# Attention and token-pair block on one core: jobs moved between attention tiles, and the last two tiles merged with the first token pair into one hand-ordered passage

## The reference

```
x = x + attention(layernorm(x))        # 16 heads of 32
x = x + ffn(layernorm(x))              # 512 -> 4096 -> 512, gate/up/down, 4-bit weights with scales
attention: q,k = rotate(silu(x Wq)), rotate(silu(x Wk)); v = x Wv
           per chunk of 128: o = (q k^T * D) v + (q*decay) S;  S = lam*S + (k*decay)^T v
           o = rmsnorm_per_head(o * sigmoid(x Wg1 Wg2)) * w;  out = o Wo
ffn:       (gelu(x Wg^T) * (x Wu^T)) Wd^T
```

## Time and profile before

| | us |
|---|---|
| median of 3 runs | 1325.35 (1324.91 to 1329.5) |
| profiled execution, its own time | 1327.92 |
| its span | 1325.8 |
| PE busy | 1287.1 (97%) |
| DVE busy | 945.0 (71%) |
| ACT busy, POOL busy | 475.7, 434.4 |
| mean granted clock of PE | 0.99 |

### The profile page before, as it was taken

The page is one execution under the profiler, slowest core; times in us unless marked ns, Lnnn a source line. Parts: engine busy times, 40 slices in busy tenths (PEclk is TensorE's granted clock), DMA queues, the critical chain, the costliest instruction groups (busy, mean ns, idle before and its releaser), DMA issues.

```text
span 1325.8 us, 19563 instructions
## 1 busy us (share of the span) xinstructions
PE 1287.1 (97%) x6796; PEld 1058.3 (80%) x6796; DVE 945.0 (71%) x1618; ACT 475.7 (36%) x799; POOL 434.4 (33%) x360
## 2 busy tenths in 40 slices
PE   8799999998789999999999999999999999999998
PEld 6688777886578888888888888888888888888887
DVE  7687988778666676667676676667676676767665
ACT  4333343333443323333333333333433333333331
POOL 2233554465442223232423223232413222232410
PEclk9799999998999999999999999999999999999999
DMA  9000000000010110000000010000000100100003
GB/s 318 8 1 10 12 14 1 1 2 0 1 33 16 32 32 28 27 24 24 24 32 16 32 32 24 32 24 24 24 32 16 32 31 17 38 24 24 24 9 119
DMA packets 21774, 40.17 MB, mean 30 GB/s; under 512 B 2660, under 2 KB 2916, under 8 KB 21604
## 3 DMA queue, kind: packets, MB, share of 16 engines
q1 hardware_dynamic: 21060, 39.47, 9.1%
q10 hardware_dynamic: 672, 0.13, 0.0%
HBM read 35.40 MB, written 4.19 MB: 30 GB/s over the span
## 4 chain that ended last, share of the span: by engine, by line
PE 90%; DVE 7%; issue 2%; ACT 1%; DVEq 0%; ACTq 0%
PE bank L1293 15%; PE bank L1296 15%; PE bank L1295 15%; PE bank L1151 12%; PE bank L1153 12%; PE bank L1152 12%; PE bank L1165 2%; PE bank L1241 1%; PE bank L1258 1%; DVE nt_t L597 1%; PE bank L1398 1%; DVE xol L791 1%; PE bank L1248 1%; DVE nt_t L599 1%; PE bank L1281 1%
## 5 line engine op out<-in xcount | busy, mean ns | idle before, releaser
L881 DVE TENSOR_TENSOR acc<-acc,bank 128x512 f32<-128x512 f32 x248 | 169.4, 683 | 129.2 <-PE bank L1153 129.2
L1151 PE MATMUL bank<-wdh,hh 128*128 128x512 f32 x512 | 199.3, 389 | 0.0
L1153 PE MATMUL bank<-wdh,hl 128*128 128x512 f32 x512 | 199.2, 389 | 0.0
L1152 PE MATMUL bank<-wdl,hh 128*128 128x512 f32 x512 | 199.2, 389 | 0.0
L1293 PE MATMUL bank<-xoh,wgh 128*128 128x512 f32 x448 | 175.9, 393 | 4.8 <-DVE xol L791 2.4
L1293 PE MATMUL bank<-xoh,wuh 128*128 128x512 f32 x448 | 175.1, 391 | 0.7 <-ACT cxa L494 0.7
L1296 PE MATMUL bank<-xoh,wgl 128*128 128x512 f32 x448 | 174.5, 390 | 0.0
L1296 PE MATMUL bank<-xoh,wul 128*128 128x512 f32 x448 | 174.3, 389 | 0.0
L1295 PE MATMUL bank<-xol,wuh 128*128 128x512 f32 x448 | 174.3, 389 | 0.0
L1295 PE MATMUL bank<-xol,wgh 128*128 128x512 f32 x448 | 174.3, 389 | 0.0
L897 DVE TENSOR_TENSOR hl<-hx,hh 128x512 fp32r<-128x512 f32 x128 | 114.5, 895 | 52.1 <-ACT hh L501 51.7
(11 more groups left out here) (156 smaller groups left out, 2341.5 us busy)
## 6 DMA issues: line engine op xcount, KB each, us to landing
stg<-packed_dram SPq DMA_DIRECT2D x48, 256.0 KB, 2.6
stg<-scales_dram SPq DMA_DIRECT2D x48, 256.0 KB
out_dram<-acc SPq DMA_DIRECT2D x16, 256.0 KB, 2.0
acc<-x_dram SPq DMA_DIRECT2D x3, 1024.0 KB, 14.7
w_in<-wq_dram SPq DMA_DIRECT2D x2, 512.0 KB, 5.2
w_in<-wk_dram SPq DMA_DIRECT2D x2, 512.0 KB, 6.9
w_in<-wv_dram SPq DMA_DIRECT2D x2, 512.0 KB, 8.8
w_in<-wo_dram SPq DMA_DIRECT2D x2, 512.0 KB, 11.1
```

The source lines that it names most:

```text
L881: V.tensor_tensor(row, row, BY[j % 2][:], ALU.add).then_inc(y_add, 1)
L1151: pe.matmul(dst, w_h, x_h, start=start, stop=False)
L1152: pe.matmul(dst, w_h, x_l, start=False, stop=False)
L1153: return pe.matmul(dst, w_l, x_h, start=False, stop=stop)
```

## The change

Nothing is computed differently; PE, DVE, ACT and POOL issue the same products. What is different:

1. **Jobs between tiles.** Bits, scales and parts of the three units go from tiles (4,6,8), (5,7,9), (6,8,10) to (3,6,9), (5,7,10), (6,8,11). The five bit steps stay together, ahead of `gated`. LN1 statistics: tiles 2 and 3 now ahead of the low part of x of tile 1, bn_stats of 4 to 7 in the same place before the loop, 8 to 11 aggregated in tile 4, 12 to 15 in tile 8 (before: 8 to 15 in tile 4). `norm1(2)` goes ahead of the silu of tile 1 and `wo_hi` into tile 0, behind `norm1(3)`. LN2 statistics are cut at rows 0, 8, 13, 15, 16 instead of 0, 8, 14, 16; the second part is in tile 13.
2. **Passage.** Tiles 14 and 15 and pair (0,0) are one piece of code per engine, with x1's groups spread in it. The loop of pairs starts at (0,1).
3. **x1.** The row pairs are taken in the order 2, 0, 1, 3, 4 ... 7; the first is staged in a new buffer `xst`, then `ws` and `stg` in turn, and the banks are `X1_BANKS`. Some attention results go to other banks (Wo products to bank 3, the state's product to bank 2).
4. Buffers stand in another order in memory.

```diff
-LN2_ROWS = (0, 8, 14, 16)
-UNIT_BITS, UNIT_SCALE, UNIT_PARTS = (4, 6, 8), (5, 7, 9), (6, 8, 10)
+LN2_ROWS = (0, 8, 13, 15, 16)
+X1_ORDER = (2, 0, 1, 3, 4, 5, 6, 7)
+X1_BANKS = (0, 6, 1, 0, 6, 1, 0, 6, 1, 0, 6, 1, 0, 6, 1, 0, 5, 2, 5, 2, 5, 7, 5, 7, 5, 7, 5, 7, 5, 7, 5, 6)
+UNIT_BITS, UNIT_SCALE, UNIT_PARTS = (3, 6, 9), (5, 7, 10), (6, 8, 11)
...
+            xst = sb("xst", [P, 2 * OPS * P], F32, att_w)
+        x_stage = [xst[:]] + 4 * [ws[:].rearrange("p a s m -> p (a s m)"), stg[:]]
...
@@ ACT, start @@
+            norm1(2, 2)
             silu_qk(1)
             gate_low(1)
-            norm1(2, 2)
-            wo_hi()
...
@@ DVE, start @@
+            dve.wait_ge(s_x[0], 16)
+            stats(2, 4)
+            stats_r(2, 4, 1)
             xt_lo_(1)
             gate_low(0)
...
-            dve.wait_ge(s_x[0], 16)
-            stats(2, 4)
-            stats_r(2, 4, 1)
+            dve.wait_ge(s_x[1], 16)
+            stats(4, 8)
...
@@ DVE, tile @@
-                if t == CHUNKS:
-                    stats_r(2 * CHUNKS, TILES, 3)
+                if t == 4:
+                    stats_r(8, 12, 3)
+                if t == 5:
+                    dve.wait_ge(s_x[3], 16)
+                    stats(12, 14)
+                if t == 7:
+                    stats(14, 16)
+                if t == 8:
+                    stats_r(12, 16, 4)
                 if t == 11:
                     stats2(0)
-                if t == 14:
+                if t == 13:
                     stats2(1)
...
@@ POOL, x1_sums(n), i = X1_ORDER[n] @@
+                if n >= 3:
+                    pool.wait_ge(x1t_ps, 4 * n - 4)
+                pool.wait_ge(s_r2, (1, 1, 1, 1, 2, 3, 3, 4)[i])
...
@@ DVE, new @@
+            def passage():
+                s, t = TILES - 2, TILES - 1
+                normed(s - 1)
+                decayed_q(s)
+                gate_low(t)
+                ot_lo_(s - 1)
+                rope_of(BATCH - 1, s % CHUNKS, t, t % CHUNKS)
+                masked(s)
+                x1(0, 3)
+                gated(s)
+                x1(4, 5)
+                normed(s)
+                x1(6, 6)
+                add_x1(s - 1)
+                x1(7, 7)
+                state(BATCH - 1, s % CHUNKS, BS[0])
+                x1(8, 8)
+                ot_lo_(s)
+                x1(9, 9)
+                decayed_q(t)
+                x1(10, 12)
+                masked(t)
+                x1(13, 17)
+                gated(t)
+                normed(t)
+                add_x1(s)
+                ot_lo_(t)
+                stats2(2)
...
+                x1(18, 19)
...
+                add_x1(t)
+                x1(20, 20)
+                stats2(3)
+                x1(21, 21)
...
@@ PE, new @@
+            def passage():
+                s, t, b = TILES - 2, TILES - 1, BATCH - 1
+                c = t % CHUNKS
+                qk_transpose(s)
+                k_project(t)
+                gate1(t)
+                o_transpose(s - 1)
+                pe.wait_ge(st_done, kvs(b, c - 1))
+                v_project(t)
...
+                for g in range(KT):
+                    scores(g)
+                pe.wait_ge(qk_silu, t + 1)
+                x1(0, 0)
+                pe.wait_ge(ot_lo, s)
+                inter()
+                pe.wait_ge(v_sb, t + 1)
+                x1(1, 2)
+                intra(s, c - 1)
+                x1(3, 3)
+                gate2(t)
+                x1(4, 4)
+                o_back(s)
+                x1(5, 6)
+                for k in range(KT):
+                    o_part(k, BS[1])
+                x1(7, 7)
+                kv_product(b, c - 1, BS[0])
+                x1(8, 8)
+                o_transpose(s)
+                x1(9, 10)
+                pe.wait_ge(x1_done, s)
+                pe.wait_ge(st_done, kvs(b, c))
+                qk_transpose(t)
...
```

More of the change, by code:

```diff
@@ L503, in pair @@
+            batches(act, tile, passage)
             def pair(q, p):
                 P_ = 2 * q + p
-                first = isinstance(q, int) and P_ == 0
                 ready = isinstance(q, int) and q == 0
                 last = isinstance(q, int) and q == BLOCKS - 1
-                def x1(*groups):
-                    if first:
-                        for g in groups:
-                            x1t_hi_(g)
                 act.wait_ge(g_ps, 7 * P_ + 1)
@@ L516, in pair @@
                 copy(hx[C11][:], GA, g_copy)
-                if not first:
-                    wait(act, y_ps, 8 * P_ - 8)
-                    high_of(C22, P_ - 1)
+                wait(act, y_ps, 8 * P_ - 8)
+                high_of(C22, P_ - 1)
                 if p == 1 and not ready:
@@ L729, in stats2 @@
                 dve.wait_ge(ln2_done, last)
-                newton(s_ntl, ln2[:, rows, 1], last - first, r2[:, rows], NT * (4 + n), 1.0,
+                newton(s_ntl, ln2[:, rows, 1], last - first, r2[:, rows], NT * (5 + n), 1.0,
                        LN_EPS)
@@ L915, in pair @@
+            batches(dve, tile, passage)
             def pair(q, p):
                 P_ = 2 * q + p
-                first = isinstance(q, int) and P_ == 0
                 ready = isinstance(q, int) and q == 0
                 last = isinstance(q, int) and q == BLOCKS - 1
-                def x1(*groups):
-                    if first:
-                        for g in groups:
-                            x1t_lo_(g)
                 def y(j):
-                    if not first:
-                        add_y(P_ - 1, 1 - p, j)
@@ L930, in pair @@
-                done = ready and P_ <= 1
-                if not done:
+                    add_y(P_ - 1, 1 - p, j)
+                if not ready:
                     up_22(P_ - 1)
@@ L1116, in tile, with passage @@
                     down_lo(DOWN)
-                if 12 <= t <= 14:
+                if 12 <= t <= 13:
                     x1_sums(t - 12)
-            def last_tile():
-                x1_sums(3)
-                x1_sums(4)
-                x1_sums(5)
-                x1_sums(6)
-                x1_sums(7)
-            batches(pool, tile, last_tile)
+            def passage():
+                rope_b_(TILES - 1, CHUNKS - 1)
+                scaled(BATCH - 1, CHUNKS - 2)
+                for n in range(2, 8):
+                    x1_sums(n)
+            batches(pool, tile, passage)
             def pair(q, p):
-                P_ = 2 * q + p
-                first = isinstance(q, int) and P_ == 0
                 ready = isinstance(q, int) and q == 0
@@ new lines, in passage @@
+                inter()
+                x1(14, 15)
+                pe.wait_ge(prob_sb, QB * t + QB)
+                x1(16, 16)
+                intra(t, c)
+                x1(17, 17)
+                pe.wait_ge(x1t_lo, 16)
+                pe.wait_ge(dq_lo, 2)
+                gate(GA, A11, 0, B11, True)
+                o_back(t)
+                for k in range(KT):
+                    o_part(k, BS[1])
+                x1(18, 18)
+                gate(GB, A12, 0, B21, True)
+                x1(19, 19)
@@ new lines, in passage @@
+                pe.wait_ge(g_copy, 1)
+                gate(GA, S2, 0, T2, False)
+                o_transpose(t)
+                gate(GC, S1, 0, T1, True)
+                pe.wait_ge(g_copy, 2)
+                gate(GA, S3, 0, T3, False)
+                pe.wait_ge(ot_lo, t + 1)
+                pe.wait_ge(xg_done, t + 1)
+                for k in range(KT):
+                    o_part(k, BS[2])
+                pe.wait_ge(g_copy, 3)
+                gate(GA, A22, 0, T4, False)
+                x1(20, 20)
@@ new lines, in passage @@
+                up(UC, S1, 0, T1, True)
+                x1(25, 25)
+                pe.wait_ge(u_copy, 2)
+                up(UA, S3, 0, T3, False)
+                x1(26, 27)
+                pe.wait_ge(u_copy, 3)
+                up(UA, A22, 0, T4, False)
+                x1(28, 29)
+                pe.wait_ge(u_sum, 2)
+                up(UC, S4, 0, B22, False)
+                x1(30, 30)
+                pe.wait_ge(h_gelu[C12], 1)
+                x1(31, 31)
+            batches(pe, tile, passage)
@@ L1519, in pair @@
                 gate(GA, A22, p, T4, False)
-                if first:
-                    o_ready(TILES - 1)
-                    for k in range(KT):
-                        o_part(k, BS[2])
                 rows(1)
@@ L1580, in blocks @@
 def blocks(eng, pair):
-    pair(0, 0)
     pair(0, 1)
```

508 lines of the change are left out of this document (237 added, 271 removed).

## The result

The changed kernel takes 1308.9 us (median of 4 runs, 1306.1 to 1309.9), the kernel before beside it 1325.1; ratio 0.9873, 95% interval 0.9849 to 0.9896. The prediction was 1307.4. The profiled executions lie further apart than the medians: 1327.9 against 1306.1, spans 1325.8 and 1304.0. So the changed kernel has a second profiled execution (experiment 1, span 1308.7), and every stage is read in both. The table gives each stage of PE's timeline as after minus before; borders are the starts of the scores of tiles 2, 6, 8 and 11 (80.93, 156.43, 195.15, 252.73 us before), T (299.19) and the second pair (380.14).

The account below looks back on a forecast made before the run. PE, busy 97% of the span, was taken as the bound, with only its idle and slow clock to win. Five terms, -8.5 - 1.8 + 1.1 + 3.2 - 12.0 = -18.0, took 1325.35 to 1307.4 us; range 1299 to 1317.

Parts of the forecast that it names:

- Place 1: Tiles 0 and 1: earlier scores outweigh a new 2.8 us idle ahead of gate2; -8.5 us, bounds -3 and -10.5.
- Rival 2: The start gains only 3 us, from late landing or half clock from 25 to 36 us: 1312.9 us; chance 12%.
- Place 2: Tile 4: fewer statistics and no bits remove PE's wait; -1.8 us, bounds -2.0 and -0.5.
- Places 3 and 4: Tiles 6 and 8: bits, or statistics beside POOL remainders, delay gating; waits 2.2 and 3.5 us, cost +1.1 and +3.2 us.
- The down unit at 11 finds 2 us or more ... nothing: Tile 11: the down unit's parts find 2 us or more before PE's next wait, so they cost nothing.
- Place 5: Passage from tile 14's qk transposes (T) to the second pair: 68.5 us instead of 80.9; -12.0 us, bounds -17 and -5.
- floor 62.3 us: Passage: PE's work without 16.0 us idle and 2.6 us lost to slow clock in 320 to 331 us.
- at the head: Start of the passage: tile 13's sq transposes, now ahead of tile 15's V, wait 1.4 us for sq.
- the DVE chain from T+21 to T+27: Passage: tile 14's norm, add, state update and remainders 6 to 9 on DVE make PE wait 3.2 us.
- Just met: Passage: POOL's sixth-row sum gives first parts at T+48.5, PE wants them at T+49.2, so no wait.
- Rivals 1 and 3: DVE bounds the passage, gain 5, 1314.4, 17%; collisions in tiles 6 and 8 free, passage 3 us idle, 1300, 9%.
- Rival 4: Passage: many short waits each drop the clock, with all of it at half +50 us, 1357; chance 3%.

Follow-up runs that it names:

- experiment 1: The changed kernel run again with no edit, for a second profiled execution: 1309.7 us, ratio 0.9869.
- the start alone: Kernel before with only the changed kernel's new start (statistics of tiles 2 and 3, norm of tile 2 and output weight copies moved): 1322.2 us, ratio 0.9951.
- experiment 5: Changed kernel with its start and tiles 1 to 12 as in the kernel before, so only the passage is new: 1312.4 us, ratio 0.9877.
- the third kernel of experiments 8 to 10: Changed kernel with early wide copies and remainders, bits in tiles 3, 7, 9, parts 6, 8, 10, statistics of tiles 12 to 15 in tile 5: 1300.1 us.
- the first of these: Changed kernel with bits in tiles 3, 7, 10, parts 6, 9, 11, statistics of tiles 12 to 15 in tile 5, first LN2 statistics in tile 12: 1306.3 us.
- experiments 6 and 7: Changed kernel with tile 15's V again ahead of tile 13's sq transposes: 1308.8 us; changed kernel with row 13's LN2 statistics alone and early: 1309.8 us.
- second kernel of experiments 8 to 10: Changed kernel with only the first two units' wide copies and POOL remainders earlier: 1302.5 us, ratio 0.9834.
- experiment 11: Changed kernel with x of tiles 2 and 3 issued earlier, early remainders, middle jobs spread again, second unit's bits in tile 5: 1298.1 us, ratio 0.979.

## Why the prediction was right, and where it was not

- **Place 1** held. Idle of 2.8 us, landing near 19.5 to 20.1 and -8.5: measured 1.74 to 4.01 us, 19.05 to 20.31, and -8.3 in the mean. The 1.5 us off for a slow clock, which the first execution alone would have refuted (clock 1.00), belongs there: 0.82 in four of the eight, 0.67 in one. By the medians the start alone brought less, 5.6 us; its profiled execution has 5.9 at tile 2. Rival 2's late landing is no case against it but one end of the same spread.
- **Place 2**: -2.6 against -1.8, past its bound of -2.0. With the wait went its 1.37 + 0.48 us and the issue gap of 0.17 behind it, and tile 5 became 0.35 us shorter, which I had not priced.
- **Places 3 and 4**: the waits came out 0.3 us shorter than forecast (1.93, 3.25). Clock loss varied: 0 and 2.4 us behind tile 6, 0.7 and 1.7 behind tile 8.
- **"The down unit at 11 finds 2 us or more ... nothing"** failed: +1.4 us there. I had counted DVE's free time ahead of the gating, but LN2's first statistics take it in tile 11, and POOL's parts of the down unit then stretch the steps behind it. Either alone shows no wait (the statistics in experiment 5 and in the third kernel of experiments 8 to 10, the parts in the first of these). It is the collision of places 3 and 4, in a tile where I had not looked for it.
- **Place 5**: floor 62.3 us, measured 60.0. The term that was mis-sized is the slow clock of before: PE's work took 64.9 - 60.0 = 4.9 us longer, not 2.6. In 320 to 331 us nearly all 7.2 us of work, and not 5.2, ran at the granted clock of 0.53, which makes 3.4 us; the other 1.5 us stay open. That term is why both executions gained 14 to 15 and not 12. Waits 6.2 forecast, 6.8 and 5.7 measured, and they fell where forecast: 1.04 at the head (1.4), 2.9 in the DVE chain from T+21 to T+27 (3.2), 0.46 for tile 15's masks (0.5), 0.48 and 0.80 at the end (1.1). (The five terms given for that chain add up to 8.3 us, not to the 9.8 between T+17.2 and T+27; the forecast of the waits doesn't use the difference.) "Just met" at T+49 was right (no wait there). The wait ahead of the transposes at T+56, 1.56 us in the first execution alone, has another holder than its row says: LN2's steps of row 15, stretched beside POOL's sums to 4.4 us in the first execution and 3.0 in the second, with the remainder behind them that frees the bank:

```profile
342.83 0.28 DVE L624 SCALAR_TENSOR_TENSOR nt_t<-r 128x1 f32<-128x1 f32 x1
...
345.55 0.59 DVE L627 SCALAR_TENSOR_TENSOR r<-nt_t,r 128x1 f32<-128x1 f32 x1
346.18 0.65 DVE L750 SCALAR_TENSOR_TENSOR nm<-ln,r 128x1 f32<-128x1 f32 x1
346.75 0.68 DVE L831 TENSOR_TENSOR xol<-bank,xoh 128x512 fp32r<-128x512 f32 x1
```

  That reading is by the times (PE's 347.58 follows 346.75 + 0.68; 351.72 follows 350.88 + 0.69); no run took these steps away. PE's transposes there read `ws`, and the POOL instruction that the row names writes `stg`.
- Rivals 1 and 3 fall: the passage gained 14 to 15 us, not 5, with DVE busy for 55.9 of 66.8 us, and the collisions in tiles 6 and 8 are there. Rival 4 falls as a price, not as a mechanism: the clock is 1.00 in the passage of nine of the ten executions that have it unaltered, but in the third kernel of experiments 8 to 10 it fell behind the same waits of 0.82 and 1.02 us (PE's work 61.3 us instead of 60.0), and in experiments 6 and 7 it fell as well. The sum came within 1.5 and 2.3 us of the two medians (1308.9, 1309.7) partly since errors cancelled: +1.8 us in tile 11 and after against 2 to 3 us too little in the passage. Some of that nearness is luck: the same kernel's profiled gain was 21.8 us in one execution and 17.1 us in the other.

## What to carry to other kernels

Price a job in the slack of the engine that does it and in that of the engine it disturbs: POOL's remainders were free on POOL and cost PE 1.1 us alone, 1.9 to 3.3 with DVE work beside them, and nothing once they ran where DVE had time. A short wait that lets another engine's queue start earlier can cost nothing (without its 1.0 us PE waited 1.3 and 0.9 us more at two later places, and the medians were the same). And where the start depends on when one transfer lands, one profiled execution is one draw: move the transfer before tuning what follows it.

## What the runs showed of the hardware

- Which DVE instructions POOL holds. Beside POOL's first remainder bn_stats on 128x512 kept its time (0.69), beside the second the SCALAR_TENSOR_TENSOR with two SBUF inputs took 2.46 instead of 0.69. The Trainium skill (SBUF — State Buffer, Who interferes with whom) says that an instruction with at most one SBUF input, outside the two-port modes, does not contend; the row of bn_stats agrees. The one-input TENSOR_SCALAR of 0.44 us between the two (150.13 to 150.57) tells little, since POOL's first remainder ended and its second began just there. Other one-input instructions were held: the step L620 (128x16, 1.89 us instead of 0.17) and L717 in experiment 11 (1.27 instead of 0.44); whether by such a mode, no run here tells.
- Granted clock behind an idle of PE ahead of the first gate2 (25.6 to 35 us): 1.00 after 0.23, 1.26, 1.28, 1.74, 1.86 and 1.93 us; 0.82 after 2.03, 2.17, 2.34 and 2.81; 0.67 after 4.01; 0.54 after 6.35. Behind tile 6 the same 1.93 us left it at 1.00 in one execution and brought it to 0.50 (167 to 172 us) in another. Behind tile 8 it fell after 1.42 us (second kernel of experiments 8 to 10) and not after 1.38 (third). So the length of one idle alone doesn't tell whether the clock falls.
